# A two-layer graph network on one core: edge copies and checks moved off VectorE, class 0's weighted windows ahead of the LayerNorm statistics, h0's turning later

## The reference, cut to what matters

```python
h = jnp.maximum(_layernorm(x, axis=-1), 0.0)
# three times: m = concat([h[dst], h[src] - h[dst]]) @ W + b;  h = relu(segment_sum(m, dst) / max(cnt, 1))
x = x + _L0_gnn_ref(h, edge_index, ...)
h = jnp.maximum(_layernorm(x, axis=-1), 0.0)
# agg = segment_sum(edge_weight * (h @ W)[src], dst);  relu(batchnorm(agg + bias))
x = x + _L1_gnn_ref(h, edge_index, edge_weight, 625, ...)
```

## Time and profile before

| | us |
|---|---|
| median of 3 runs | 115.23 (115.13 to 115.28) |
| the profiled execution's own time | 115.68 |
| its span in the trace | 113.8 |
| TensorE products busy | 100.1 (88%) |
| TensorE loads busy | 91.9 (81%) |
| VectorE busy | 93.0 (82%) |
| ScalarE busy | 57.6 (51%) |
| GpSimd busy | 19.7 (17%) |

### The profile page before, as it was taken

How to read it: one execution, slowest core, us unless ns; L and a number is a source line. 1 busy time by engine, 2 the same in 40 slices (tenths; PEclk the granted TensorE clock), 3 DMA queues, 4 the chain that set the end, 5 groups by cost and what they waited for, 6 DMA issues and landing times.

```text
span 113.8 us, 2667 instructions
## 1 busy us (share of the span) xinstructions
PE 100.1 (88%) x1031; PEld 91.9 (81%) x1031; DVE 93.0 (82%) x269; ACT 57.6 (51%) x142; POOL 19.7 (17%) x27
## 2 busy tenths in 40 slices
PE   0399999799999999998899999998999979999650
PEld 0335898686998899987899999997999969989440
DVE  2399999999999999999976699667899799246960
ACT  2497999997897591125507135506133236050530
POOL 7100000000000197600291700750000000000000
PEclk9999999999999999999999999999999999999955
DMA  2978810000300000000413000000000000000044
GB/s 40 228 212 164 296 32 0 0 6 3 92 6 6 0 9 6 0 0 3 129 56 95 3 0 0 0 6 0 0 6 0 0 0 0 0 0 9 0 111 114
DMA packets 5402, 4.63 MB, mean 41 GB/s; under 512 B 556, under 2 KB 5387, under 8 KB 5387
## 3 DMA queue, kind: packets, MB, share of 16 engines
q1 hardware_dynamic: 4460, 3.68, 12.0%
q10 hardware_dynamic: 926, 0.75, 2.6%
HBM read 3.79 MB, written 0.64 MB: 39 GB/s over the span
## 4 chain that ended last, share of the span: by engine, by line
PE 45%; issue 21%; DVE 16%; ACT 7%; POOL 5%; DMA 3%; SPq 0%; POOLq 0%; DVEq 0%
PE bank L1082 10%; PE bank L1332 9%; PE bank L1084 9%; PE bank L1083 9%; DMA edge_rows_i<-in_dst_dram 3%; POOL parts L477 2%; POOL own L486 2%; DVE stats L531 2%; PE bank L1372 2%; PE bank L1145 2%; DVE h_lo L748 1%; PE bank L1417 1%; PE bank L1232 1%; DVE stats L859 1%; PE bank L1123 1%
## 5 line engine op out<-in xcount | busy, mean ns | idle before, releaser
L578 DVE TENSOR_SCALAR src_hot<-node_id,edge_cols 125x626 f16<-125x626 f16 x77 | 23.5, 381 | 0.0
L1232 PEld LDWEIGHTS bank<-dst_hot,src_hot 125*128 125x128 f16 x505 | 19.0, 98 | 3.1 <-DVE src_hot L578 1.7
L1232 PE MATMUL bank<-dst_hot,src_hot 125*128 125x84 f16 (+6 forms) x505 | 20.3, 195 | 1.2 <-DVE src_hot L578 0.9
L1332 PE MATMUL bank<-counts,u_lo 125*128 125x312 f32 (+1 forms) x60 | 16.3, 308 | 0.0
L1024 ACT ACTIVATE h_hi<-pre 128x312 fp32r<-128x312 f32 (+1 forms) x12 | 5.6, 468 | 18.1 <-DVE pre L742 18.1
L1332 PE MATMUL bank<-counts,u_hi 125*128 125x312 f32 (+1 forms) x48 | 14.0, 307 | 0.0
L477 POOL TENSOR_TENSOR parts<-parts 125x625 f32<-125x625 f32 x5 | 6.4, 1298 | 43.2 <-DVE src_hot L578 36.1
L1332 PEld LDWEIGHTS bank<-counts,u_lo 125*128 125x128 f32 x60 | 10.9, 189 | 0.0
L967 ACT ACTIVATE parts<-bank 125x250 f32<-125x250 f32 x25 | 10.3, 417 | 0.0
L1332 PEld LDWEIGHTS bank<-counts,u_hi 125*128 125x128 f32 x48 | 9.1, 189 | 0.0
L891 ACT ACTIVATE counts<-bank 125x125 fp32r<-125x125 f32 (+1 forms) x25 | 7.5, 302 | 2.0 <-PE bank L1232 2.0
(11 more groups left out here) (138 smaller groups left out, 252.5 us busy)
## 6 DMA issues: line engine op xcount, KB each, us to landing
raw<-in_L_gnn_W_dram SPq DMA_DIRECT2D x3, 512.0 KB, 7.0
x_in<-in_x_dram ACTq DMA_DIRECT2D x1, 560.0 KB
raw<-in_L_gnn_Wf_dram SPq DMA_DIRECT2D x1, 512.0 KB, 3.8
wf<-in_L_gnn_Wf_dram SPq DMA_DIRECT2D x1, 256.0 KB, 8.1
raw<-in_L_gnn_Wf_dram SPq DMA_DIRECT2D x1, 256.0 KB, 2.7
raw<-in_L_gnn_W_dram SPq DMA_DIRECT2D x1, 256.0 KB, 4.7
out_dram<-x_in SPq DMA_DIRECT2D x1, 224.0 KB
out_dram<-x_in SPq DMA_DIRECT2D x1, 168.0 KB
```

The costliest lines, as they stand in the source:

```text
L578: dve.tensor_scalar(src_hot[:, t % RING, 0:IDS], node_id[:, 0:IDS], edge_cols[:, 0, t:t + 1], None, ALU.is_equal).then_inc(src_hot_vector, 1)
L1232: return pe.matmul(built[s][:, :, n0:n0 + n], src_hot[:, t % RING, BLK * s:BLK * s + P], dst_hot[:, c, :, j // 2, c0:c0 + n, j % 2], start ...
L1332: ins = pe.matmul(bank[KF * h + f][:, 0:e - a], u[:, k, P * f:P * (f + 1)], counts[0:BLK, k, a:e], start=False, stop=(k == NB - 1 and u is ...
```

## The change

What it does, part by part:

- The group "edges" becomes two: "dst" (bank 5, read by `rel`) and "src" (bank 6). TensorE turns dst first, each with its own signal. ScalarE, not VectorE, copies the sources to `edge_cols`; the targets are copied no more (in the general path they are made from `rel` and `base_id`).
- The group "parts" moves to bank 5, so its filling waits for `rel`; its third product pair, the sum of the parts, goes. ScalarE, not VectorE, copies the parts to `weight_parts`. Its copy of the weights to `parts_f` moves from there to behind the root.
- The check of the windows goes to GpSimd in two operations, the sum of the parts in one, and the copy to `degree_r` too. VectorE keeps the comparison with the weights and the maximum, and does them before tile 21 (`CHECK_AT`).
- VectorE makes the weighted window of class 0 before the statistics, and `scale_shift` before tile 3 (`SHIFT_AT`), so that tile 2, the one of the first three that is its own, stands between the statistics and the wait for the root.
- ScalarE's early tiles are 0 and 1 in place of 0 and 4. It copies `vecs` too, after the last block of h0.
- `keep_warm(4)` in place of 10. h0's turning is before tiles 5, 6, 8 and 11 (both last blocks) in place of 2, 4, 6 and 9; `turn_vecs` before tile 7 in place of 5; the first neighbour terms before tile 10 in place of 8.

```diff
--- before.py
+++ after.py
@@ -61,9 +61,9 @@
...
 FULL = 112
-SCALAR_EARLY, SCALAR_NEXT, SCALAR_LATER = (0, 4), (22, 27), {0: (34, 38), 1: (52,), 2: (71,)}
+SCALAR_EARLY, SCALAR_NEXT, SCALAR_LATER = (0, 1), (22, 27), {0: (34, 38), 1: (52,), 2: (71,)}
 SCALAR_TILES = SCALAR_EARLY + SCALAR_NEXT + sum(SCALAR_LATER.values(), ())
-VECS_AT, DIFF_AT = 13, 33
+SHIFT_AT, CHECK_AT, DIFF_AT = 3, 21, 33
 U_AT = (30, 38, 42)
@@ -290,6 +290,8 @@
...
         edge_cols_ready = sem("edge_cols_ready")
+        parts_checked = sem("parts_checked")
+        slow_cols_ready = sem("slow_cols_ready")
         row_parts_ready = sem("row_parts_ready")
@@ -369,9 +371,10 @@
...
         groups.spare = (5, 6, 7)
-        groups.plan(["edges"], edge_cols_ready, 1)
+        groups.plan(["dst"], rel_ready, 1, banks=(5,))
+        groups.plan(["src"], edge_cols_ready, 1, banks=(6,))
         groups.plan(["weights"], weight_cols_ready, 1, banks=(7,))
-        groups.plan(["parts"], weight_parts_ready, 2)
+        groups.plan(["parts"], weight_parts_ready, 1, banks=(5,))
         groups.plan([("h0", b) for b in range(2)], h0_t_ready, 1, banks=(7, 5))
@@ -464,6 +467,18 @@
...
                                base=-DEGREE, pattern=[[0, P]], channel_multiplier=1).then_inc(constants_ready, 1)
+            pool.wait_ge(constants_ready, 4)
+            pool.tensor_copy(degree_r[:, :], degree_f[:, :]).then_inc(degree_ready, 1)
+            by_class = lambda t: t.rearrange("p (c j) -> p c j", c=NB)
+            pool.wait_ge(padding_ready, 2)
+            pool.wait_ge(rel_ready, 1)
+            step.add(pool.tensor_scalar(by_class(dev[:, 0, :]), rel[:, :, 0:PER], -(WINDOW - 1) / 2, None, ALU.add))
+            step.wait()
+            pool.tensor_tensor(by_class(dev[:, 0, :]), by_class(dev[:, 0, :]), window_scale[:, :, :],
+                               ALU.mult).then_inc(parts_checked, 1)
+            pool.wait_ge(weight_parts_ready, 1)
+            pool.tensor_tensor(by_class(dev[:, 1, :]), weight_parts[:, :, 0, 0:PER], weight_parts[:, :, 1, 0:PER],
+                               ALU.add).then_inc(parts_checked, 1)
@@ -553,13 +568,11 @@
...
-            groups.wait_filled(dve, "edges")
-            e2 = groups.bank["edges"][0:EP, 0:2 * TILES].rearrange("p (v t) -> p v t", v=2)
+            groups.wait_filled(dve, "dst")
             dve.wait_ge(constants_ready, 3)
             dve.wait_ge(padding_ready, 2)
-            dve.tensor_tensor(rel[:, :, 0:PER], e2[:, 1, :].rearrange("p (c j) -> p c j", c=NB),
+            dve.tensor_tensor(rel[:, :, 0:PER], groups.bank["dst"][0:EP, 0:TILES].rearrange("p (c j) -> p c j", c=NB),
                               base_id[:, :, 0:PER], ALU.subtract).then_inc(rel_ready, 1)
-            dve.tensor_copy(edge_cols[:, :, :], e2).then_inc(edge_cols_ready, 1)
@@ -593,33 +606,24 @@
...
             plain_window(0)
-            groups.wait_filled(dve, "parts")
-            p3 = groups.bank["parts"][0:EP, 0:3 * TILES].rearrange("p (v t) -> p v t", v=3)
-            p2 = groups.bank["parts"][0:EP, 0:2 * TILES].rearrange("p (v c j) -> p c v j", v=2, c=NB)
-            dve.tensor_copy(weight_parts[:, :, :, 0:PER], p2).then_inc(weight_parts_ready, 1)
-            dve.wait_ge(weight_cols_ready, 1)
-            dve.scalar_tensor_tensor(out=dev[:, 1, :], in0=parts_f[:, 0, :], scalar=WEIGHT_SCALE, in1=p3[:, 2, :],
-                                     op0=ALU.mult, op1=ALU.not_equal).then_inc(weight_parts_ready, 1)
-            step.add(dve.scalar_tensor_tensor(out=dev[:, 0, :].rearrange("p (c j) -> p c j", c=NB), in0=rel[:, :, 0:PER],
-                                              scalar=-(WINDOW - 1) / 2, in1=window_scale[:, :, :], op0=ALU.add,
-                                              op1=ALU.mult))
-            step.wait()
-            dve.wait_ge(weight_parts_ready, 2)
-            dve.tensor_reduce(dev_max[:, :], dev[:, :, :].rearrange("p v t -> p (v t)"), AX.X, ALU.max,
-                              apply_absolute_value=True).then_inc(dev_ready, 1)
+            dve.wait_ge(weight_parts_ready, 1)
+            weighted_window(0)
             dve.wait_ge(x_loaded, 32)
...
             variances(range(NB))
-            weighted_window(0)
-            scale_shift(range(NB), norm_ready)
             dve.wait_ge(edge_cols_ready, 1)
             for t in range(TILES):
-                if t == VECS_AT:
-                    groups.wait_filled(dve, "vecs")
-                    dve.wait_ge(constants_ready, 4)
-                    dve.tensor_copy(vecs[:, :], groups.bank["vecs"][:, 0:6 * KF]).then_inc(vecs_ready, 1)
-                    dve.tensor_copy(degree_r[:, :], degree_f[:, :]).then_inc(degree_ready, 1)
+                if t == SHIFT_AT:
+                    scale_shift(range(NB), norm_ready)
+                if t == CHECK_AT:
+                    dve.wait_ge(parts_checked, 2)
+                    dve.wait_ge(weight_cols_ready, 1)
+                    step.add(dve.scalar_tensor_tensor(out=dev[:, 1, :], in0=parts_f[:, 0, :], scalar=WEIGHT_SCALE,
+                                                      in1=dev[:, 1, :], op0=ALU.mult, op1=ALU.not_equal))
+                    step.wait()
+                    dve.tensor_reduce(dev_max[:, :], dev[:, :, :].rearrange("p v t -> p (v t)"), AX.X, ALU.max,
+                                      apply_absolute_value=True).then_inc(dev_ready, 1)
                 if t % PER == PER - 2 and t // PER + 1 < NB:
@@ -678,6 +682,9 @@
...
                 dve.memset(slow_hot[:, IDS:IDS + 1], 1.0)
+                dve.tensor_tensor(edge_cols[:, 1, :].rearrange("p (c j) -> p c j", c=NB), rel[:, :, 0:PER],
+                                  base_id[:, :, 0:PER], ALU.add).then_inc(slow_cols_ready, 1)
+                dve.wait_ge(slow_cols_ready, 1)
                 dve.memset(parts[:, len(EARLY_SUMS):NB, :, 1, :], 0.0)
@@ -895,8 +902,12 @@
...
             nc.scalar.activation(row_parts[:, 0, :], weight_rows[:, :], ACT.Copy, scale=WEIGHT_SCALE).then_inc(row_high_ready, 1)
-            groups.wait_filled(act, "weights")
-            copy(parts_f[:, 0, :], groups.bank["weights"][0:EP, 0:TILES]).then_inc(weight_cols_ready, 1)
+            groups.wait_filled(act, "src")
+            copy(edge_cols[:, 0, :], groups.bank["src"][0:EP, 0:TILES]).then_inc(edge_cols_ready, 1)
+            groups.wait_filled(act, "parts")
+            act.wait_ge(padding_ready, 1)
+            p2 = groups.bank["parts"][0:EP, 0:2 * TILES].rearrange("p (v c j) -> p c v j", v=2, c=NB)
+            copy(weight_parts[:, :, :, 0:PER], p2).then_inc(weight_parts_ready, 1)
@@ -946,12 +957,15 @@
             root(rstd[0:BLK, 0:NB], moments[0:BLK, 0:NB, 1])
+            copy(parts_f[:, 0, :], groups.bank["weights"][0:EP, 0:TILES]).then_inc(weight_cols_ready, 1)
             act.wait_ge(norm_ready, 1)
...
                     h0_high(b - 1)
+            groups.wait_filled(act, "vecs")
+            copy(vecs[:, :], groups.bank["vecs"][:, 0:6 * KF]).then_inc(vecs_ready, 1)
             source_tile(SCALAR_NEXT[0])
@@ -1096,21 +1110,19 @@
...
             pe.wait_ge(edge_rows_ready, 1)
-            o = fill("edges")
-            for v in range(2):
-                ins = pe.matmul(o[0:EP, TILES * v:TILES * (v + 1)], edge_rows[:, v, :], ident_h[:, :], start=True, stop=True)
-            ins.then_inc(filled, 1)
+            for v, name in ((1, "dst"), (0, "src")):
+                pe.matmul(fill(name)[0:EP, 0:TILES], edge_rows[:, v, :], ident_h[:, :], start=True,
+                          stop=True).then_inc(filled, 1)
             pe.wait_ge(edge_weights_loaded, 16)
...
             o = fill("parts")
-            for at, part, opens, closes in ((0, 0, True, True), (1, 1, True, True), (2, 0, True, False), (2, 1, False, True)):
-                ins = pe.matmul(o[0:EP, TILES * at:TILES * (at + 1)], row_parts[:, part, :], ident_h[:, :],
-                                start=opens, stop=closes)
+            for v in range(2):
+                ins = pe.matmul(o[0:EP, TILES * v:TILES * (v + 1)], row_parts[:, v, :], ident_h[:, :], start=True, stop=True)
             ins.then_inc(filled, 1)
...
             pe.wait_ge(padding_ready, 1)
-            keep_warm(10)
+            keep_warm(4)
@@ -1207,7 +1219,7 @@
...
-            jobs = {2: (0,), 4: (1,), 6: (2,), 9: (3, 4)}
+            jobs = {5: (0,), 6: (1,), 8: (2,), 11: (3, 4)}
             assert max(jobs) < len(window_pieces(0))
@@ -1236,9 +1248,9 @@
...
                     for i in range(len(pieces)):
-                        if i == 5:
+                        if i == 7:
                             turn_vecs()
-                        if i == 8:
+                        if i == 10:
                             neighbour_terms_0(U0_BLOCKS[:1])
```

## The result

The changed kernel takes 116.74 us (median of 4 runs, 116.58 to 116.85) against 115.25 us for the kernel before: a ratio of 1.0128, 95% interval 1.0111 to 1.0146. It is slower by 1.5 us; the forecast was 115.3 with a range to 115.9. The profiled execution's span is 114.5 us, against 113.8 before. Run by run the span of the changed kernel is 114.5 to 115.1 us. Runs more than 1.5% above the fastest of the same kernel, four in all, are left out of the medians, spans and ratios in the table further down.

A forecast was written before the change was run, and what follows sets the result against it. VectorE's full list was taken to bound the build: 0.62 us added before tile 21 less 0.50 gained gives +0.12, carried from the profiled 115.68 to the median 115.23, so 115.35, rounded 115.3; range 114.8 to 115.9.

The forecast's parts named there:

- What bounds the build: Whole build: VectorE is full and the build ends when its loop ends; TensorE's lateness costs nothing up to 0.67 us.
- The sum over VectorE's list: VectorE's list up to tile 22: 0.62 added before tile 21 less 0.50 gained by tile 13, +0.12 us.
- wait 0.52: VectorE before the weighted window: it idles 0.52 us until ScalarE has copied the parts.
- reciprocal at 9.55: VectorE after ScalarE's root: the reciprocal starts at 9.55 us, as before, after an idle of 0.41.
- Comparison and maximum: VectorE before tile 21: the two operations come back there, 0.28 and 0.34, 0.62 us, covered by nothing.
- +0.12 for tile 30's place: VectorE's loop: every tile from 22 on starts 0.12 us later than in the kernel before.
- the step on `keep_warm`: TensorE's warm-up, six products fewer: it rests from 7.3 us; rows alone do not say the clock is up at 10.2.
- the case: Slower rival, the clock: TensorE places tiles from 10.2 us on at 1.2 GHz, ending 0.5 later at 115.7 us; chance 0.15.
- +0.5 for a rise at 15 us: Clock rival's price: a rise 4.8 us after 10.2 makes TensorE 1.0 late, and the build ends 0.5 us later.
- TensorE's slack of 0.67 at tile 33: TensorE before tile 33: it stood 0.67 us for VectorE's one-hot, so lateness up to that costs nothing.
- The last of the prediction's signs of being wrong: TensorE at tile 33: its wait gone or ended by ScalarE's tile 34, with products after 12 us at twice their durations.
- The faster rival: VectorE before the reciprocal: the wait for the root is shorter than 0.41, gaining up to 0.4 us; chance 0.25.

The follow-up runs named there:

- its control: The kernel before, unaltered, run in the place of a changed kernel against the kernel before: 115.51 us, ratio 1.0016 (0.9998 to 1.0034).

## Why the prediction was wrong

**What bounds the build** held. VectorE's list sets its end: 0.44 us taken from it came out of the span as 0.4, its 1.40 us of delay is nearly all of the 1.5, and a TensorE 1.0 us late did not go into the span.

**The sum over VectorE's list** held in size. Forecast: window at 6.21, wait 0.52, reciprocal at 9.55, loop at 9.85; measured 6.18, 0.48, 9.44, 9.74, of which 0.09 each is only the earlier arrival of the edge rows. The windows before tile 15 start at 13.26, before at 13.86: from the casts 0.51 earlier, against a forecast of 0.50. Comparison and maximum took 0.51 (16.07 to 16.58), not 0.62. So +0.12 for tile 30's place becomes nothing. With seven warm-up products, where nothing else is late, VectorE's loop ends 34.97 us after its cast begins; in the kernel before it was 34.98. With ten the ratio is 1.0007. The forecast was right for the change without its `keep_warm(4)`; between +0.12 and nothing the times cannot decide.

**What failed is the step on `keep_warm`**, twice. First the chance: it was written that by the rows alone nothing says that the clock is up at 10.2, and the case got 0.15. But the rows pointed one way: in the kernel before the clock rose only near 9.5, at the end of ten products at half speed, and the forecast's own list takes six away and lets TensorE rest, as it then did for 1.6 us (0.16, 1.25 and 0.20) before 10.2. The kernel before with four shows that this alone costs 1.1% of the time, of which 0.7 us is in the span. By the Trainium skill's page TensorE: Matmul & The Clock Gate, section What's actually happening, cited for that rival, activity releases the throttle; the runs agree, with products at half speed to 14 us and later after four alone, and at full speed by some 11.2 us in every profiled run with ten. The rise is not at one place even so: it was near 9.5 us in the kernel before and near 11 us in its control, where two turnings at 10.56 still took 0.68 us.

Second the price, +0.5 for a rise at 15 us. TensorE's slack of 0.67 at tile 33 was set against the lost work, and the sentence "VectorE stays the one with work" was taken to close the case. The turnings were followed to ScalarE, and ScalarE to tile 34 only, its slack there 0.24. They were not followed on to VectorE before tile 30, where the high part of u is read. ScalarE's list is full from 10 to 20 us, so what comes to it late goes out late. At tile 30 the slack was 18.72 - 17.58 = 1.14 us and the high part of u was 2.34 later, so the wait is 1.2 by this working and 1.31 measured. From the casts the high part is 2.43 later; VectorE begins 0.11 after it ends (19.92 to 20.03), which leaves 1.03 of slack, and the difference is the 1.40 by which VectorE is late. The range, to 115.9, ended below a median of 116.74 for that reason. The last of the prediction's signs of being wrong came true: TensorE's wait at 24.38 is ended by ScalarE's tile 34, and products after 12 us take half as long again or more (3.10 us for 1.97).

**The faster rival** got its condition and not its gain. The wait for the root was 0.19 (9.25 to 9.44) and not 0.41, but not because the root came much sooner: from the casts the reciprocal is 0.02 us from the forecast (9.53 against 9.55, in the kernel before's times). VectorE came later to it, chiefly because the weighted window took 0.15 longer in its slot (0.72 for 0.57). A shorter wait in front of the same root wins nothing. That rival's figures also have a slip: 115.23 - 0.4 is 114.83, as its range says, and the 114.95 beside it belongs to -0.29.

## What to carry to other kernels

Starting TensorE's useful products earlier by cutting its warm-up won nothing here: tile 0 began 2.0 us sooner (3.45 us after VectorE's cast instead of 5.48) and VectorE waited 1.31 us at tile 30. Shortening a warm-up is a change of its own, to be timed alone before it is joined with others. When one engine may run at half speed, go through every reader of everything it writes, and ask of each how late it may be: a slack at one wait says nothing of the next. And where one engine's list is full, look for its own idle stretches and move its work into them: 0.44 us of work moved so came out of the span as 0.4.

## What the runs showed of the hardware

GpSimd's small operations were longer than the forecast of 0.2 to 0.3 us, and the window beside them was longer too. GpSimd's timeline of the changed kernel, and the weighted window of class 1, with GpSimd at rest, on VectorE:

```profile
5.42 0.58 POOL L475 TENSOR_SCALAR dev<-rel 125x85 f32<-125x85 f16 x1 [1.65 <-DVE rel L574]
6.08 0.36 POOL L477 TENSOR_TENSOR dev<-dev,window_scale 125x85 f32<-125x85 f32 x1
6.40 0.77 POOL L480 TENSOR_TENSOR dev<-weight_parts 125x85 f32<-125x85 f16 x1
```

```profile
13.71 0.68 DVE L587 TENSOR_TENSOR dst_hot<-dst_hot,weight_parts 125x1008 f16<-125x1008 f16 x1
```

Class 0's window, at 6.18 beside the last two of these, took 0.80, in the other profiled runs of the changed kernel and its variants as well; the same work took 0.68 with GpSimd at rest, and 0.65 in the kernel before at 8.98. GpSimd's three operations took 0.58, 0.36 and 0.77, each beside a window of VectorE for part of its time. No run has them alone, so that they were lengthened too is not shown. The Trainium skill's page Advanced Engine Details and Errata, section GPSIMD Details, says that GpSimd shares an SBUF read and a write interface with VectorE and conflicts with its instructions of two SBUF inputs. The window has two SBUF inputs and its 0.80 agrees; no run took the GpSimd operations away, so the cause is argued and not shown. It cost nothing here, since the wait for the root lay behind it.
